# 64-wide linear attention: the whole triangle of scores by key tile, with a decay table by distance, in place of chunks and a state

## What is computed

```python
qkv = silu(h @ qkv_w.T)                   # 32 heads of 64: q, k, v
# per head, in blocks of 32, with slope s of the head and state = 0:
aw = einsum('bhid,bhjd->bhij', qi, ki) * dd        # exp(-s * (i - j)) for i >= j, else 0
y = einsum('bhij,bhjd->bhid', aw, vi) + einsum('bhid,bhde->bhie', qi * qd, state)
state = state * bd + einsum('bhsd,bhse->bhde', ki * kd, vi)
out = sigmoid(h @ gate_w.T) * rmsnorm(y) * norm_w @ out_w.T
```

## Time and profile before

| | |
|---|---|
| median of 3 runs | 3193.43 us (3193.4 to 3193.88) |
| the profiled execution | 3191.56 us |
| its span, first to last instruction | 3188.7 us |
| mean granted clock of TensorE | 0.929 |
| the changed layer in the span | about 1597 to 2483 us |

### The profile page before, as it was taken

The page is one execution under the profiler, slowest core; times in us unless marked ns, Lnnn a source line. Parts: engine busy times, 40 slices in busy tenths (PEclk is TensorE's granted clock), DMA queues, the critical chain, the costliest instruction groups (busy, mean ns, idle before and its releaser), DMA issues. The chain is left out here.

```text
span 3188.7 us, 46399 instructions
## 1 busy us (share of the span) xinstructions
PE 2822.7 (89%) x15610; PEld 1928.5 (60%) x15610; DVE 1675.7 (53%) x4583; ACT 827.0 (26%) x1344; POOL 974.7 (31%) x1089
## 2 busy tenths in 40 slices
PE   7999999998999999999979999999999538888872
PEld 3444458885556555788757777777777423443451
DVE  5566646666564655466644333333335556555555
ACT  2333344442101011444422222222221002222210
POOL 0000036775444444667721222222221001212200
PEclk8999999999999999999989999999998757887885
DMA  3000020000000000100000000000000000000000
GB/s 137 1 0 0 0 99 1 0 0 1 1 0 0 0 0 0 80 0 0 0 14 14 14 1 14 14 14 1 14 1 1 23 0 1 1 0 0 0 0 26
DMA packets 6281, 37.88 MB, mean 12 GB/s; under 512 B 272, under 2 KB 4368, under 8 KB 4496
## 3 DMA queue, kind: packets, MB, share of 16 engines
q1 hardware_dynamic: 6160, 36.34, 2.9%
HBM read 34.24 MB, written 2.10 MB: 11 GB/s over the span
## 5 line engine op out<-in xcount | busy, mean ns | idle before, releaser
L590 PE MATMUL banks<-back 32*128 32x512 f32 (+3 forms) x1088 | 366.3, 603 | 30.0 <-DVE back L600 20.7
L365 PE MATMUL banks<-moe_parts 128*128 128x512 f32 x1536 | 369.9, 397 | 13.8 <-POOL moe_parts L445 8.9
L817 ACT ACTIVATE back<-banks 128x1024 f32<-128x1024 f32 (+3 forms) x256 | 217.1, 863 | 460.9 <-PE banks L711 460.6
L365 PEld LDWEIGHTS banks<-moe_parts 128*128 128x128 f32 x1536 | 289.1, 192 | 77.2 <-issue 18.9
L1433 PE MATMUL banks<-lin_parts 128*128 128x512 f32 x1152 | 305.9, 411 | 19.3 <-DVE lin_parts L1684 15.5
L1619 DVE TENSOR_TENSOR ffn_pack<-banks,back 128x512 f32<-128x512 f32 x128 | 88.4, 691 | 351.0 <-PE banks L1446 350.9
L711 PE MATMUL banks<-back 32*128 32x512 f32 (+3 forms) x1024 | 242.2, 585 | 20.6 <-DVE back L833 12.5
L1433 PEld LDWEIGHTS banks<-lin_parts 128*128 128x128 f32 x1152 | 212.5, 193 | 67.2 <-issue 21.0
L590 PEld LDWEIGHTS banks<-back 32*128 32x128 f32 x1088 | 135.8, 200 | 185.7 <-DVE back L604 77.7
L1749 POOL TENSOR_TENSOR ffn_pack<-ffn_pack 128x256 f32<-128x256 f32 x112 | 82.9, 741 | 497.2 <-ACT ffn_pack L1582 497.2
L604 DVE TENSOR_REDUCE back<-banks 128x1 f32<-128x512 f32 x272 | 176.3, 686 | 80.2 <-PE banks L590 75.5
(11 more groups left out here) (224 smaller groups left out, 5235.7 us busy)
## 6 DMA issues: line engine op xcount, KB each, us to landing
back<-p_raw SPq DMA_DIRECT2D x8, 1024.0 KB, 4.8
back<-p SPq DMA_DIRECT2D x1, 7696.0 KB, 21.2
ffn_pack<-ffn SPq DMA_DIRECT2D x1, 6144.0 KB, 26.7
back<-p SPq DMA_DIRECT2D x1, 5152.0 KB, 15.0
back<-p SPq DMA_DIRECT2D x2, 1792.0 KB, 8.0
out<-x SPq DMA_DIRECT2D x1, 2048.0 KB, 7.5
x<-x_in SPq DMA_DIRECT2D x1, 1536.0 KB, 12.7
small_pack<-small SPq DMA_DIRECT2D x1, 619.0 KB, 4.9
```

What stands on the lines that cost most here:

```text
L365: mm = nc.tensor.matmul(bank[:], up[:, n % 2, a, which, kd, :], xp[:, b, kd, :], start=((a, b, kd) == (0, 0, 0)), stop=((a, b, kd) == (1, ...
L590: nc.tensor.matmul(bank[:, 0:n], qs[head_rows[j], hg, qi * P:(qi + 1) * P], ks[head_rows[j], hg, 0:n], start=True, stop=True).then_inc(D.f ...
L817: nc.scalar.activation(pt[:, (kt % 2) * 2 + pair, :, q0:T], two[:, :, q0:T], ACT.Exp, scale=0.25).then_inc(A.free.s, 2)
```

## The change

The layer has no chunks, no state, no turned or decayed k and no decayed q. For a key tile n of 128 keys and a pair r of heads, the scores with **all** queries from n * 128 on are made at once (2 matmuls, up to 512 columns each), multiplied with a table of exp(-s * distance) that is the same for every key tile (its first 512 - 128 n columns are used), and the values are added up over the key tiles in one PSUM bank. A unit has 8 steps (r, n) in place of 4. The products are issued one half at a time, one for each step; the projection in two parts, in steps 2 and 4. Ring S has two bank pairs, ring O is not used, the projection goes through ring D. The square and the gate are done once for each r over 512 columns. The table of a quad (1 MB) is double-buffered and loaded by SyncE: the first two in the layer before, the others behind the weights of a quad.

```diff
-    kd_ = sb("kd", [P, 2, NT, P])
...
+    decay = take(2 * DEC5).rearrange("p (u h i) -> p u h i", u=2, h=4)
...
-    steps = [(w, n) for w in range(N) for n in range(NT)]
+    steps = [(w, r, n) for w in range(N) for r in range(2) for n in range(NT)]
...
+    PRODUCTS = (("q", 0), ("k", 0), ("q", 1), ("k", 1), ("v", 0), ("v", 1), ("gate", 0), ("gate", 1))
+    SPLITS = {2: 0, 3: 1, 5: 2, 7: 3}
...
+            def scores(w, r, n):
                 if n == 0:
-                    pe.wait_ge(A.free.s, A.released(0, "k", w, 1))
+                    pe.wait_ge(A.free.s, A.released(0, "k", w, r))
                 pe.wait_ge(S.free.s, S.may_fill(0))
+                pair = S.fill("scores", w, r, n)
+                for h, rows_ in enumerate(halves):
+                    mm = nc.tensor.matmul(pair[:, h, 0:T - n * P], kt[rows_, w % 2, r, n * P:(n + 1) * P],
+                                          qs[rows_, w % 2, r, n * P:T], start=True, stop=True)
                 mm.then_inc(S.full.s, 1)
 
-            def grow_state(w, n):
...
+            def output(w, r, n):
+                if (r, n) == (0, 0):
+                    pe.wait_ge(A.free.s, A.released(0, "v", w, 1))
+                pe.wait_ge(S.free.s, S.released(0, "scores", w, r, n))
+                if n == 0:
+                    pe.wait_ge(U.free.s, U.may_fill(0))
+                    U.fill("out", w, r)
+                bank = U.banks[0]
+                for h in range(2):
+                    head = 2 * r + h
+                    mm = nc.tensor.matmul(bank[halves[h], n * P:T], vs[:, w % 2, n, head * D5:(head + 1) * D5],
+                                          am[:, n % 2, h, 0:T - n * P], start=(n == 0), stop=(n == NT - 1))
                 if n == NT - 1:
+                    mm.then_inc(U.full.s, 1)
...
+            for k, (w, r, n) in enumerate(steps):
+                s = r * NT + n
+                for what in product_in(w, s):
                     product(*what)
+                if s in (2, 4) and w:
+                    project(w - 1, s // 2 - 1)
+                if s == 6 and w > N - B:
                     mean_square(w - 1 - (N - B))
                 if k + 1 < len(steps):
                     scores(*steps[k + 1])
-                grow_state(w, n)
-                output(w, n)
+                output(w, r, n)
...
+                if n == NT - 1:
+                    act.wait_ge(U.full.s, U.may_read(0))
...
+                    nc.scalar.activation(to, bank[:], ACT.Square).then_inc(c.sq_taken.s, 1)
...
+            def decay_scores(w, r, n):
+                u, b = units[w]
+                if (b, r, n) == (0, 0, 0):
+                    dve.wait_ge(c.s_dec[u % 2].s, 16 * (u // 2 + 1))
+                dve.wait_ge(S.full.s, S.may_read(0))
+                pair = S.read("scores", w, r, n)
+                nc.vector.tensor_tensor(am[:, n % 2, :, 0:T - n * P], pair[:, :, 0:T - n * P],
+                                        decay[:, u % 2, 2 * r:2 * r + 2, 0:T - n * P], ALU.mult).then_inc(S.free.s, 1)
+
+            def gate(w, r):
+                dve.wait_ge(c.sq_taken.s, c.sq_taken.at(0, w * 2 + r + 1))
+                g = gt[:, w % 2, r, :]
+                nc.vector.scalar_tensor_tensor(out=g, in0=g, scalar=1.0, in1=U.banks[0][:], op0=ALU.add, op1=ALU.mult)\
+                    .then_inc(U.free.s, 1)
...
+            for k, (w, r, n) in enumerate(steps):
+                s = r * NT + n
+                if s in (2, 4) and w:
+                    add_output(w - 1, s // 2 - 1)
+                if s == 6 and w > N - B:
+                    finish(w - 1 - (N - B))
                 if k + 1 < len(steps):
                     decay_scores(*steps[k + 1])
+                if s == 6 and w > N - B:
                     scale(w - 1 - (N - B))
...
+                if n == NT - 1:
+                    gate(w, r)
...
-            def decay_q(w, n):
...
+                if n == NT - 1 and w >= B:
+                    add_squares(w, r)
...
+                if u + 1 < QUADS:
+                    sp.wait_ge(S.free.s, S.released(0, "scores", u * B - 1, 1, NT - 1))
+                    sp.dma_start(flat(decay[:, (u + 1) % 2]), c.p5_dec[u + 1]).then_inc(c.s_dec[(u + 1) % 2].s, 16)
...
+        c.S = Ring(psum[2:4], sem("score_pair_full"), sem("score_pair_free"))
...
+            for u in range(2):
+                at = n5 + RAW5 + u * DEC5
+                sp.dma_start(c.back[:, at:at + DEC5], p5_dec[u]).then_inc(c.s_dec[u].s, 16)
```

More of the change, by code:

```diff
@@ L1402, in product @@
                 u, b = units[w]
[L1403 to L1411, removed]
                 m = NAMES.index(name)
@@ L1463, in output @@
[L1463 to L1476, removed]
-                        mm = nc.tensor.matmul(bank[halves[h], to], vs[:, w % 2, n, head * D5:(head + 1) * D5],
-                                              am[:, n % 2, h, r, :], start=True, stop=True)
-                    if n:
-                        mm = nc.tensor.matmul(bank[:, to], state[:, (n - 1) % 2, r, :], qd[:, m % 2, r, :],
-                                              start=False, stop=True, skip_group_check=True)
-                mm.then_inc(U.full.s, 1)
@@ L1484, in project @@
-            def project(w):
-                u, b = units[w]
-                for half in range(2):
-                    pe.wait_ge(U.free.s, U.released(0, "out", w, 2 * half + 1))
-                    pe.wait_ge(O.free.s, O.may_fill(0))
-                    bank = O.fill("y", w, half)
-                    for i in range(2 * half, 2 * half + 2):
-                        for r in range(2):
-                            mm = nc.tensor.matmul(bank[:, (i % 2) * DM:(i % 2 + 1) * DM],
-                                                  gt[:, w % 2, r, i * P:(i + 1) * P], wo[:, 2 * u + r, :],
-                                                  start=(r == 0), stop=(r == 1))
-                    mm.then_inc(O.full.s, 1)
+                pair = S.fill("scores", w, r, n)
@@ new lines, in project @@
+            def project(w, half):
+                u, b = units[w]
+                if half == 0:
+                    pe.wait_ge(c.set_up.s, c.set_up.at(0, 2))
+                    pe.wait_ge(U.free.s, U.released(0, "out", w, 1))
+                pe.wait_ge(D.free.s, D.may_fill(0))
+                bank = D.fill("y", w, half)
+                for i in range(2 * half, 2 * half + 2):
+                    for r in range(2):
+                        mm = nc.tensor.matmul(bank[:, (i % 2) * DM:(i % 2 + 1) * DM],
+                                              gt[:, w % 2, r, i * P:(i + 1) * P], wo[:, 2 * u + r, :],
+                                              start=(r == 0), stop=(r == 1))
+                mm.then_inc(D.full.s, 1)
@@ L1512, in mean_square @@
                     for r in range(2):
-                        mm = nc.tensor.matmul(bank[:, i:i + 1], squares[:, b, r, i, :], one, start=(r == 0), stop=(r == 1))
+                        mm = nc.tensor.matmul(bank[:, i:i + 1], squares[:, b, r, i * P:(i + 1) * P], one, start=(r == 0), stop=(r == 1))
                 mm.then_inc(D.full.s, 1)
@@ L1652, in add_output @@
[L1652 to L1663 removed]
+                bank = D.read("y", w, half)
@@ L1719, in _ @@
             finish(B - 1)
-            add_output(N - 1)
+            for half in range(2):
+                add_output(N - 1, half)
             scale(B - 1)
@@ L1724, in _ @@
         def _(pool):
-            nc.gpsimd.memset(state[:], 0.0).then_inc(c.set_up.s, 1)
             pool.wait_ge(c.s_p5.s, 16)
```

254 lines of the change are left out of this document (74 added, 180 removed).

## The result

| | before | after |
|---|---|---|
| median of 4 runs each | 3193.65 us | 3246.97 us (3245.37 to 3248.92) |
| the profiled execution | 3191.56 us | 3248.5 us |
| its span | 3188.7 us | 3245.8 us |
| mean granted clock of TensorE | 0.929 | 0.933 |

The change makes the kernel **slower by 1.6%**: the ratio is 1.0163, with a 95% interval of 1.0146 to 1.0181. The forecast was 3260 us, in a range from 3242 to 3290; the rise is 53.3 us where 67.5 were forecast.

The account below looks back on a forecast made before the run. TensorE was taken to bound the layer, without gaps: +64.8 us for 31 units, -1.8 start, +3 last unit, +1.5 VectorE waits, sum +67.5 on 3191.56, so 3259, or 3260 for the median; range 3242 to 3290.

Parts of the forecast that it names:

- How TensorE is charged: TensorE blocks: a slot costs 0.107 us per 128 columns, plus 0.21 per row-tiled or 0.155 per column-tiled block.
- removed: TensorE, each unit: old scores, state, output and turned keys go, 10.18 us; 15.36 us of products and projection stay.
- added: TensorE, each unit: scores and outputs of two head pairs over the whole triangle come, 11.45 us.
- moved: TensorE, each unit: products cut into eight halves and projection in two parts take 16.18 us for 15.36.
- (a): VectorE's pass over up to 1024 score elements takes 1.24 us, stays hidden with 1.4 to spare, cost 0.
- (b): The one output bank: square and gate finish before the next pair fills it, 0.7 us to spare, cost 0.
- (d): SyncE issues 1 MB more per quad; its waits and the table loads stay hidden, cost 0.
- (e) The ends: Layer's start -1.8 us, last unit's TensorE work +3, inverse root and scaling on VectorE before a pass and gate +1.5.
- 1 (the bank binds): Output bank decides from a VectorE delay of 0.7 us; 0.5 us lost in each of 64 pairs, 3292, chance 8%.
- 2 (wide slots cheap): TensorE's 512-wide slots cost 1.6 times a 128-wide one; unit 23.5 us, kernel 3134, chance 3%.
- 3 (turns hidden): TensorE's turns of tiling, 0.365 us in each of 8 steps, vanish behind long matmuls; kernel 3170, chance 3%.
- 4 (the halves don't overlap): With one matmul for each half of TensorE's array, the halves don't overlap: +8.5 us per unit, 3525, chance 1%.

Follow-up runs that it names:

- The band: Changed kernel with scores, decay pass and values of a head pair stopped 18/slope queries behind the key tile: 3199.38 us, ratio 1.0020 to the kernel before.
- the diagonal run: Changed kernel with each key tile scoring only its own 128 queries, part of the computation left out: 3088.28 us.
- the two runs with fewer turns: Changed kernel with both halves of q, k, v, gate made together: 3221.09 us; the same plus scores, then values, of two key tiles in a row: 3188.49 us.
- the delayed gates: Changed kernel with idle VectorE passes before each gate of units 3 to 30: 3268.63 us with one pass, 3323.52 with three.
- the run with three passes: Changed kernel with three idle VectorE passes before each gate of units 3 to 30: 3323.52 us.

## Why the prediction was right, and where it was off

**How TensorE is charged, removed, added, moved: right.** Over the unit above the eight product halves sum to 12.59 us and the projection to 3.64, 16.23 together where the step "Moved" had 16.18; the scores to 5.92 and the values to 5.51, 11.43 where "Added" had 11.45. The unit is 27.66 for 27.63. "Removed" follows from 25.54 with these. The band adds the price of the columns in four more quads. The step that carried it was to take the price of a 512-wide slot from another layer's rows, and to add the turn apart from the columns; the diagonal run shows the first, the two runs with fewer turns the second.

**A rule against the rows.** The page "TensorE: Matmul & The Clock Gate" of the Trainium skill, section Back-to-back issue gap, would have had wide slots at well under their columns' price. In this case's f32 matmuls a width of 128 in two passes adds 0.21 us at every width measured (512, 384, 256, 128), so the trace does not agree.

**What must stay hidden: right.** (a) The decay pass takes 1.23 us (forecast 1.24) and nothing waits for it in the steady units. (b) The slack of the output bank is 0.73 to 0.75 us (forecast 0.7), shown by the delayed gates. (c) VectorE is busy 131.5 of 400 us. (d) The tables land in 4.9 us (median), in the page's DMA section, and the units that begin a quad are as long as the others:

```profile
back<-p_dec SPq DMA_DIRECT2D x8, 1024.0 KB, 4.9
```

**(e) The ends: wrong, and the only step that is.** *The start* was forecast at -1.8 and is -4.0. TensorE's work and waits in that interval shrink by 1.7, close to what was said. Beyond them the kernel before has 6.4 us of it at 1.2 GHz (up to 1618.9, and from 1632.5 to 1636.0) and the changed one 1.3 (up to 1618.4), which by the count above is 2.3 us. The other two traces of each kernel have the interval likewise (19.3 and 19.1 us before, 17.0 and 16.1 after). *The end* was forecast at +6.6 and is -1.8. The step priced the last unit "from 12.8 to 15.1", at +2.2 us for 2.4 GHz and +4.5 for 1.2 GHz, and took +3 for a mixture: **it assumed that both kernels meet the same clock there.** They do not. The work was right, +4.3 forecast (2.09 and 2.2) and +4.2 counted in the first traces. The clock was given +0.8 and is -6.3 (11.4 us lost before, 5.1 after). The inverse root and the scaling were given +1.5 and the waits as a whole grow by 0.4: the two that the step meant are there, 1.91 us for a gate (below) and 2.37 for a decay pass, but the last unit of the kernel before has waits of the same size, 4.2 us against 4.3, which the step left out. These are 7.1 and 1.1 of the 8.4 between forecast and measurement.

Why the clock falls in one and not in the other was not isolated; the rows show only what stands ahead of it. In the kernel before TensorE waits for VectorE and then issues 16 one-column matmuls:

```profile
2436.87 0.60 PE L1408 MATMUL banks<-small_pack,back 128*128 128x128 f32 x4
...
2438.34 1.92 PE L1513 MATMUL banks<-small_pack,ffn_pack 128*128 128x1 f32 x16 [0.87 <-DVE back L1612]
```

and the clock is at 1.2 GHz from 2441.5 on for 10.2 us and again from 2462.0 for 17.1; the second and third traces have a wait of 0.88 at the same place and the fall at 2446.3 and 2445.5. There is no such wait in the changed kernel, since nothing turned or decayed is left for TensorE to wait on, and the same 16 matmuls lie between wide blocks. In the first and third trace the clock stays up behind them:

```profile
2496.15 1.66 PE L1416 MATMUL banks<-lin_parts 128*128 128x512 f32 x6
2497.65 1.84 PE L1476 MATMUL banks<-small_pack,ffn_pack 128*128 128x1 f32 x16
2499.42 0.49 PE L1427 MATMUL banks<-back 64*128 64x128 f32 x4
```

In the second trace, though, with the same rows up to 2499.84, it falls at 2500.9 for 3.4 us and the blocks there are drawn out:

```profile
2500.43 2.56 PE L1416 MATMUL banks<-lin_parts 128*128 128x512 f32 x6
2502.92 1.79 PE L1427 MATMUL banks<-back 64*128 64x512 f32 x4
```

So no wait is needed just ahead of a fall, though the run with three passes shows falls at longer waits, and the cause of the difference between the kernels stays open.

**The rivals.** 1 (the bank binds) has the right threshold, which the steady units do not reach. In the last unit, where the scaling stands before the gate on VectorE, it binds once, in a place to which the forecast gave part of its +1.5:

```profile
2506.26 1.08 PE L1441 MATMUL banks<-ffn_pack 128*64 128x512 f32 x4 [1.91 <-DVE back L1580]
```

2 (wide slots cheap) and 3 (turns hidden) are refuted by the unit of 27.66 us and by the runs with fewer columns and fewer turns. 4 (the halves don't overlap) would have shown a 512-wide scores block above 2 us; it is 1.06.

**The size.** 53.3 us between the medians, 57.1 between the profiled spans, and 53.6 between the means of three spans each (3188.7, 3193.3, 3192.5 and 3245.8, 3248.0, 3241.5), against 67.5: the two ends account for 10.6, a little more than the 10.4 missing between the first two profiled spans. The first trace of the kernel before is the shortest of its three, and the means of three tell more: to the first q +0.3, the first interval -3.1 (forecast -1.8), the 30 units +60.0 (+62.7), the end -1.4 (+6.6), the layers behind -2.1. Counted as above, the 30 units of the first traces are +62.8 of work, -1.7 of waits and +1.5 lost at 1.2 GHz; by the means it is +63.2, -1.7 and -1.5, since the clock costs 4.1, 8.4 and 8.4 us there before (in the first and the last of these units) and 5.7, 5.1 and 5.6 after. The work is as forecast, and the 0.1 of the first pair of traces is luck. The range gave the ends 5 us of error, and they missed by 10.6; the total lies in it because of the 16 us kept for the blocks, which did not need them. Single executions spread over 11 us (25 of the kernel before, 3188.24 to 3199.26), and the clock's falls outside the steady units are what differs between traces.

## What to carry to other kernels

Where TensorE has no gaps, count columns times passes and, apart from them, the turns between tilings: a recurrence with few columns beat a dense triangle of fewer and wider matmuls here, and putting blocks of one tiling together won back 2.2 us of a 27.7 us unit (whether the kernel before would gain by such grouping was not tried). Grouping alone brought the new form 0.16% under the kernel before. Dropping the recurrence paid with what it makes possible, a band that leaves out what the decay has made negligible, together with that grouping: 1.9%. Do not price the ends of a layer at the clock that the old order met there, and leave room for it in the range: here it made a difference of 6 us.

## What was unexpected of the hardware

**A VectorE pass between SBUF tiles hardly moves while GpSimd works.** With both operands and the result in SBUF, a 128x512 f32 pass took 1.73 us when it began 0.10 us after a GpSimd pass of 1.28 us, and ended 0.55 us after that one; the next two of the same kind, in the run with three, took 0.64 each. The gate (2030.26) and the decay passes, which read PSUM, ran beside GpSimd at their usual 0.68 us and 1.23 us. The page "GPSIMD Engine Reference" of the Trainium skill, section Specifications, says that GpSimd shares its SBUF interfaces with VectorE and contends with instructions that have two SBUF inputs; this agrees, and the run adds that the VectorE pass loses about 1.1 us of GpSimd's 1.28, more a lock than a share. Which one loses went by which began first: where the VectorE pass began 0.23 us ahead, GpSimd's took 1.73 us in place of 1.28 and VectorE's 0.83 (2060.97, output bank).

**Turns of tiling add up exactly.** Four blocks of full-array matmuls less gave 0.84 us, two scores blocks joined 0.19, two values blocks joined 0.16, and the sum of these over a unit is the measured 2.24 us.

**The same program meets different clocks.** In the 26 units in the middle of the layer all three traces of a kernel agree to 0.01 us in a unit; the 30 units with the ones around them took 779.5, 783.3 and 783.1 us in the kernel before; at the layer's end the time at 1.2 GHz was 13.7, 23.1 and 13.7 us in the changed kernel, and the layers behind it took 704.3, 704.2 and 697.6 us.
